# A four-layer graph network on one core: fewer small matmuls, and TensorE's stage work moved to 22 common lots

## What is computed

```python
# layer 0: additive attention; adj is both the projection W and the score bias
s1 = h @ W1.T; s2 = h @ W2.T                       # 256 features each
pre = s1[:, :, None, :] + s2[:, None, :, :] + b_lin
e = einsum('bije,e->bij', leaky_relu(pre, 0.2), a) + adj
x = x + sigmoid(softmax(e, axis=2) @ h)
# layer 1: xh = elu(h @ Wi + bi); e = sigmoid(tgt_i + src_j + be) * mask
# recv = elu(concat(e @ xh, xh * rowsum(e)) @ Wn + bn)
# x = x + concat(recv, xh) @ Wm + bm
# layer 2: attention exp(8 tanh(q k / 8 sqrt(d))) * adj, normalised, times h and v
# layer 3: five steps of a gated recurrent unit over messages adj @ h
```

## Time and profile before

| | before |
|---|---|
| median of three runs | 5996.21 us |
| profiled execution: time | 5989.9 us |
| profiled execution: span from first to last instruction | 5988.1 us |
| TensorE's granted clock, mean | 0.996 |
| PE (TensorE matmuls) busy | 98% |
| ACT (ScalarE) busy | 88% |
| POOL (GpSimd) busy | 82% |
| DVE (VectorE) busy | 81% |
| DMA traffic | 36.62 MB, 6 GB/s on average |

### The profile page before, as it was taken

The page is one execution under the profiler, slowest core; times in us unless marked ns, Lnnn a source line. Parts: engine busy times, 40 slices in busy tenths (PEclk is TensorE's granted clock), DMA queues, the critical chain, the costliest instruction groups (busy, mean ns, idle before and its releaser), DMA issues.

```text
span 5988.1 us, 128923 instructions
## 1 busy us (share of the span) xinstructions
PE 5885.9 (98%) x41812; PEld 2318.3 (39%) x41812; DVE 4837.7 (81%) x9171; ACT 5269.2 (88%) x12793; POOL 4916.4 (82%) x10392
## 2 busy tenths in 40 slices
PE   8999999999999999999999999999999999999997
PEld 2333333333334333333333333333433333333334
DVE  8978887888887888878888788888888887888873
ACT  8988898899988899888999889998889988899983
POOL 9988888888888888888888888888888888888880
PEclk9999999999999999999999999999999999999998
DMA  0000000000000000000000000000000000000000
GB/s 13 5 3 7 7 7 6 3 6 7 7 6 3 7 6 7 7 2 7 6 7 7 6 3 6 7 7 6 3 7 6 7 6 3 7 6 7 7 5 6
DMA packets 44353, 36.62 MB, mean 6 GB/s; under 512 B 4721, under 2 KB 39410, under 8 KB 43506
## 3 DMA queue, kind: packets, MB, share of 16 engines
q1 hardware_dynamic: 43506, 26.50, 1.5%
HBM read 9.71 MB, written 8.39 MB: 3 GB/s over the span
## 4 chain that ended last, share of the span: by engine, by line
PE 94%; ACT 2%; DVE 1%; POOL 1%; issue 1%; DMA 0%; SPq 0%; POOLq 0%; ACTq 0%; DVEq 0%
PE S L1015 58%; PE R L957 15%; PE S L957 6%; PE W L957 5%; PE R L1157 3%; PE PA L957 2%; ACT ring L812 2%; PE R L1165 1%; POOL ring L507 1%; PE PB L957 1%; PE S L1006 1%; PE S L1008 1%; DVE ring L613 1%; PE PB L1042 1%; PE PA L1023 0%
## 5 line engine op out<-in xcount | busy, mean ns | idle before, releaser
L507 POOL TENSOR_SCALAR ring<-W,U 128x256 f32<-128x256 f32 x9664 | 4686.4, 503 | 713.8 <-PE S L1015 642.2
L812 ACT ACTIVATE ring<-W,U 128x256 f32<-128x256 f32 x10272 | 4244.1, 503 | 13.3 <-PE S L1015 13.2
L1015 PE MATMUL S<-ring,a_window 128*32 128x512 f32 x32768 | 3750.1, 596 | 12.8 <-POOL ring L507 7.3
L613 DVE TENSOR_TENSOR ring<-U,W 128x512 f32<-128x512 f32 (+1 forms) x3840 | 3209.2, 862 | 155.5 <-PE S L1015 117.4
L1015 PEld LDWEIGHTS S<-ring,a_window 128*32 128x32 f32 x32768 | 952.2, 110 | 2269.6 <-issue 2245.4
L608 DVE TENSOR_TENSOR ring<-U,W 128x256 f32<-128x256 f32 x2464 | 993.6, 408 | 0.0
L957 PE MATMUL R<-mT,W 128*128 128x512 f32 (+1 forms) x640 | 339.1, 611 | 2.7 <-ACT mT L916 2.7
L957 PE MATMUL R<-AT,h 128*128 128x256 f32 x1260 | 316.8, 395 | 2.7 <-ACT h L928 2.1
L748 DVE SCALAR_TENSOR_TENSOR rh<-tr,h3T 128x512 f32<-128x512 f32 (+1 forms) x165 | 114.1, 692 | 240.2 <-ACT tr L919 240.2
L957 PEld LDWEIGHTS R<-AT,h 128*128 128x128 f32 x1260 | 230.4, 193 | 129.7 <-issue 100.6
L478 POOL TENSOR_TENSOR minus_mean<-mv,minus_one 128x4 f32<-128x4 f32 (+1 forms) x160 | 31.6, 197 | 272.3 <-DVE mv L676 216.8
(11 more groups left out here) (186 smaller groups left out, 4238.6 us busy)
## 6 DMA issues: line engine op xcount, KB each, us to landing
X<-in_x SPq DMA_DIRECT2D x64, 128.0 KB, 2.4
X_held<-X SPq DMA_DIRECT2D x32, 256.0 KB, 2.3
out<-OUT SPq DMA_DIRECT2D x64, 128.0 KB, 1.9
raw<-in_L_gnn_w_w SPq DMA_DIRECT2D x3, 128.0 KB
A<-in_adj SPq DMA_DIRECT2D x1, 256.0 KB, 2.7
Wn<-in_L_gnn_Wn SPq DMA_DIRECT2D x1, 128.0 KB
Wm<-in_L_gnn_Wm SPq DMA_DIRECT2D x1, 128.0 KB
rawu<-in_L_gnn_u_w SPq DMA_DIRECT2D x2, 64.0 KB
```

The lines of the kernel that those rows point to most:

```text
L507: last = gp.tensor_scalar(ring[:, place, g, half * N:(half + 1) * N], W[:, y, c], LARGEST, U[:, y, c, i:i + 1], ALU.min, ALU.max)
L613: piece = dve.tensor_tensor(ring[:, place, g:g + groups].rearrange("p g (h j) -> p g h j", h=NB), u.unsqueeze(3).to_broadcast([P, groups, ...
L812: last = act.activation(ring[:, place, g, half * N:(half + 1) * N], W[:, y, c], ACT.Relu, bias=U[:, y, c, i:i + 1], scale=-1.0)
L1015: last = pe.matmul(S[y][g * ROWS:(g + 1) * ROWS, :], a_window[:, c, ROWS - 1 - row:2 * ROWS - 1 - row], ring[:, place, g], start=False, st ...
```

## The change

1. **Layer 0's linear terms.** ScalarE's block becomes `Relu(W + U_minus)`, with `U_minus = -U` made by VectorE at the stage `evacuate`. That is the maximum less U of node i, and a term of node i alone drops out of the softmax over j. So `lin_w` is one matrix for all, one matmul with 512 columns replaces the two of `lin_w` and the one of `A_bias`, and `w_lin`, `lin_i`, `exp_bias`, `by_max` and its memsets go. A is added in VectorE's pass that finds the maximum, with one `tensor_tensor_reduce` per 256 columns that writes -(S + A) to SBUF and its minimum; ScalarE's exponential reads that.
2. **Layer 1.** GpSimd adds bm to X1 ahead of time (`X1_shifted`) and adds the two halves of the edge weights (`edge_sum`); the four matmuls with `bm_half` go, and the four of `ones` become one with 512 columns, behind a wait for GpSimd.
3. **Tables.** All stage tables move. POST and PRE get one table for each half of the turn. Distinct lots with a TensorE stage go from 34 to 22. The first matmul of a half comes on top: in the second half it stood in the same gap as a stage (table place 66, done after lot 63), now it stands alone. The planner gets 26 units more of GpSimd work, and the shares of a turn's 1024 blocks go from 401, 302 and 321 (VectorE, GpSimd, ScalarE) to 403, 298 and 323.

```diff
-POST = dict(score=5, exp=6, transpose=10, copy=11, aggregate=12, tanh=14, residual=15)
-PRE = dict(stats=40, norm=43, transpose=46, copy=49, project=57, evacuate=61)
-LN1 = dict(stats=17, norm=19, transpose=20, copy=23)
-L1 = dict(project=26, exp=28, elu=29, edge_terms=31, edge_copy=33, tanh=33, mask=36, aggregate=39, agg_copy=42, receive=44, recv_exp=45, recv_elu=47, out=49, residual=52)
-LN2 = dict(stats=56, norm=59, transpose=68, copy=70)
-L2 = dict(project=74, copy=77, scores=80, tanh=84, exp=85, mask=88, aggregate=94, residual=99)
-LN3 = dict(stats=2, norm=5, transpose=9, copy=10)
-L3_AT, L3_PERIOD = 12, 22
+POST = (dict(score=5, exp=6, transpose=10, copy=11, aggregate=14, tanh=16, residual=17),
+        dict(score=5, exp=6, transpose=12, copy=13, aggregate=16, tanh=18, residual=19))
+PRE = (dict(stats=40, norm=43, transpose=46, copy=49, project=58, evacuate=61),
+       dict(stats=40, norm=43, transpose=48, copy=50, project=56, evacuate=60))
+LN1 = dict(stats=19, norm=21, transpose=24, copy=26)
+L1 = dict(shift=23, project=32, exp=34, elu=35, edge_terms=40, edge_copy=42, tanh=42, mask=45, halves=46, aggregate=49, agg_copy=51, receive=54, recv_exp=55, recv_elu=56, out=58, residual=60)
+LN2 = dict(stats=62, norm=65, transpose=68, copy=70)
+L2 = dict(project=76, copy=78, scores=84, tanh=86, exp=87, mask=90, aggregate=98, residual=101)
+LN3 = dict(stats=2, norm=5, transpose=10, copy=11)
+L3_AT, L3_PERIOD = 14, 22
...
+    put(pool, L1, 0, shift=13, halves=13)
...
+                if t == L1["shift"]:
...
+                    need(gp, x2_ready, turn.at(1, -1))
+                    gp.wait_ge(x1_ready, turn.at(2, 0))
+                    gp.tensor_tensor(X1_shifted[:], X1[:], bm_half[:].unsqueeze(1).to_broadcast([P, 4, P]), ALU.add).then_inc(x1_shifted, 1)
+                if t == L1["halves"]:
+                    gp.wait_ge(edge_ready, pair)
+                    gp.tensor_tensor(edge_sum[:].rearrange("p (y n) -> p y n", y=2), edge[:, :, 0], edge[:, :, 1], ALU.add).then_inc(edge_halves, 1)
...
-                if p == PRE["evacuate"]:
-                    dve.wait_ge(uw_psum, value)
-                    dve.tensor_copy(lin_i[:, y], PA[:, N:N + NB])
+                if p == PRE[1 - y]["evacuate"]:
+                    dve.wait_ge(u_ready, value)
+                    dve.tensor_scalar(U_minus[:, y], U[:, y], -1.0, None, ALU.mult).then_inc(u_minus_ready, 1)
...
                     dve.wait_ge(freed[RING - 1], lots_done)
-                    dve.tensor_reduce(neg_max[:], S[y][:].rearrange("p (r j) -> p r j", r=NB), AXIS.X, ALU.max,
-                                      negate=True).then_inc(max_ready, 1)
-                    one_piece()
-                    dve.wait_ge(max_ready, value)
-
+                    need(dve, prob_ready, value - 1)
+                    dve.memset(score_carrier[:], 0.0)
                     for r in range(NB):
-                        last = dve.scalar_tensor_tensor(exp_bias[:, r:r + 1], neg_max[:, r:r + 1], lin_i[:, y, r:r + 1],
-                                                        lin_i[:, y, r:r + 1], ALU.subtract, ALU.add)
-                    last.then_inc(exp_bias_ready, 1)
+                        last = dve.tensor_tensor_reduce(neg_score[:, r], S[y][:, r * N:(r + 1) * N], A[:, r], -1.0, LARGEST,
+                                                        ALU.add, ALU.min, accum_out=neg_max[:, r:r + 1])
+                    last.then_inc(max_ready, 1)
...
-                    act.wait_ge(u_ready, turn.at(2, y + 1))
+                    act.wait_ge(u_minus_ready, turn.at(2, y + 1))
...
-                                          bias=U[:, y, c, i:i + 1], scale=-1.0)
+                                          bias=U_minus[:, y, c, i:i + 1])
...
-                    for r in range(NB):
-                        pe.matmul(S[y][:, r * N:(r + 1) * N], lin_w[:, y, r], H0T[:, y], start=r == 0, stop=False,
-                                  skip_group_check=True)
-                    pe.matmul(S[y][:].rearrange("p (r j) -> p r j", r=NB), ident[:], A_bias[:], start=False, stop=False,
+                    pe.matmul(S[y][:].rearrange("p (r j) -> p r j", r=NB), lin_w[:],
+                              H0T[:, y].unsqueeze(1).to_broadcast([P, NB, N]), start=True, stop=False,
                               skip_group_check=True)
...
-                    for r in range(NB):
-                        mm(PA[:, N + r:N + r + 1], H0T[:, y, r * P:(r + 1) * P], w_lin[:, 0:1])
...
-                    for y in range(2):
-                        for r in range(NB):
-                            last = mm(S[1][:, y * N:(y + 1) * N], ones[:], edge[:, y, r], r == 0, r == NB - 1)
-                    last.then_inc(agg1_psum, 1)
+                    pe.wait_ge(edge_halves, pair)
+                    mm(S[1][:], ones[:], edge_sum[:]).then_inc(agg1_psum, 1)
...
-                        mm(S[1][:, n * P:(n + 1) * P], ones[0:1, :], bm_half[:], True, False)
-                        mm(S[1][:, n * P:(n + 1) * P], recvT[:, n * P:(n + 1) * P], Wm[:, 0], False, False)
+                        mm(S[1][:, n * P:(n + 1) * P], recvT[:, n * P:(n + 1) * P], Wm[:, 0], True, False)
```

More of the change, by code:

```diff
@@ L85, in put @@
             costs[at + table[name]] += cost
[L87 to L92, removed]
+    for h in range(2):
+        half = h * LOTS_B
+        put(vector, POST[h], half, score=7, transpose=1.5, residual=3.4)
+        put(scalar, POST[h], half, exp=10, copy=4.8, tanh=5)
+        put(vector, PRE[h], half, stats=5.5, evacuate=0.6)
+        put(scalar, PRE[h], half, norm=5, copy=2.6, evacuate=12)
+        put(pool, PRE[h], half, stats=20)
     for ln in (LN1, LN2, LN3):
@@ L131, in spare_blocks @@
     spare = [0] * LOTS
-    for half in (0, LOTS_B):
-        for at in (POST["score"], POST["transpose"], PRE["stats"]):
-            spare[half + at] += 1
+    for h in range(2):
+        for at in (POST[h]["score"], POST[h]["transpose"], PRE[h]["stats"]):
+            spare[h * LOTS_B + at] += 1
     for at in (LN1["stats"], LN2["stats"], LN3["stats"], L1["elu"], L1["recv_elu"], L2["residual"]):
@@ L172, in node @@
     return half * P + g * ROWS + row
[L175 to L181, removed]
 def gnn_stack(nc, x, adj, L0_b, L0_a, L1_Wi, L1_bi, L1_We, L1_be, L1_Wn, L1_bn, L1_Wm, L1_bm, L2_q, L2_k, L2_v,
@@ L258, in gnn_stack @@
         Wm = sb("Wm", [P, 2, P])
-        bm_half = sb("bm_half", [1, P])
+        bm_half = sb("bm_half", [P, P])
         cols = sb("cols", [P, 7])
@@ L275, in gnn_stack @@
         U = sb("U", [P, 2, EC, N])
+        U_minus = sb("U_minus", [P, 2, EC, N])
         W = sb("W", [P, 2, EC, N])
-        lin_i = sb("lin_i", [P, 2, NB])
         ring = sb("ring", [P, RING, GROUPS, NB * N])
@@ L287, in gnn_stack @@
         neg_max = sb("neg_max", [P, NB])
-        exp_bias = sb("exp_bias", [P, NB])
         row_sum = sb("row_sum", [P, NB])
@@ L463, in _ @@
                              pattern=[[-1, P]], channel_multiplier=1).then_inc(gp_const, 1)
-            gp.memset(by_max[:], 1.0).then_inc(mask_ones, 1)
-            gp.wait_ge(mask_ones, 1)
-            for y in range(2):
-                for c in range(EC):
-                    for n in range(BLOCKS):
-                        g, half = group_half(n)
-                        for first, end in scalar_runs(y, c, n):
-                            last = gp.memset(by_max[:, c, y, half, g * ROWS + first:g * ROWS + end], 0.0)
-            last.then_inc(mask_set, 1)
             gp.wait_ge(dve_const, 1)
@@ L517, in body @@
                         blocks(turn, t)
-                    if p == PRE["stats"] and turn.has_main and (y == 0 or turn.pre_next):
+                    if turn.has_l12:
+                        layer1(t, turn)
+                    if p == PRE[y]["stats"] and turn.has_main and (y == 0 or turn.pre_next):
                         pre(turn.at(2, y + 2))
@@ L996, in lot @@
                 if p == 0:
-                    need(pe, prob_ready, turn.at(2, y - 1))
+                    need(pe, max_ready, turn.at(2, y - 1))
                     if y == 0:
@@ L1106, in layer2 @@
                     pe.wait_ge(hT_ready[1], pair)
-                    pe.wait_ge(prob_ready, turn.at(2, 1 if turn.has_main else 0))
+                    pe.wait_ge(max_ready, turn.at(2, 1 if turn.has_main else 0))
                     mm(S[0][:], G[:], h2T[:])
```

100 lines of the change are left out of this document (45 added, 55 removed).

## The result

The changed kernel takes 5821.18 us in the median (5805.18 to 5829.51), the kernel before beside it 5998.4: a ratio of 0.970 with a 95% interval of 0.967 to 0.973. The forecast was 5730, range 5700 to 5800. The direction was right and the size was not: 266 us were forecast and 177 came. The profiled execution took 5805.18 us (span 5803.3), against 5989.9 before and 5724 forecast for it.

A forecast was written before the change was run, and what follows sets the result against it. TensorE, busy 98% of the span, was taken as the bound: 30 turns x 9.0 us = 270, plus 8 at the edges, less 12 for stalls, net 266, so 5996.2 becomes 5730 us; range 5700 to 5800.

The forecast's parts named there:

- The working of TensorE's time: Steady turn on TensorE: fewer matmuls and merged visits remove 9.0 us, bounds 7.9 and 9.4.
- The linear terms: Layer 0's visit on TensorE: one 512-column matmul remains, 0.86 us goes twice, 1.72 us a turn.
- the output stage: TensorE's stage of 4.21 us loses the `bm_half` matmuls: 2.2 us goes, leaving about 2.
- the merged visits: TensorE's stage visits: 11 fewer a turn at 0.30 us each, 3.3 us, between 2.2 and 3.7.
- GpSimd's wait for the ring: GpSimd's wait for TensorE to free a ring place: down from 21.4 us a turn to about 10.
- The wait for `edge_halves`: TensorE behind its lot 46: costed at nothing; forecast wrong if it ends a TensorE wait.
- the gap at the turn's change: TensorE before a looped turn's first matmul: the prediction gave it no term and no rival.
- The sign of being wrong that I had set: Profile after: forecast wrong if steady turns are over 179 us; 175 to 176 us expected.
- what VectorE's operations cost: VectorE in a steady turn: grows by at most some 2 us, to 152.5.
- the rival "GpSimd is held by VectorE": U_minus on VectorE may hold GpSimd's blocks some 1 us a turn; no change of the sum, no chance given.
- The term of 0.4 us a turn: Turn's change, lots 0 to 8: ScalarE's lead touches zero, costing 0.4 us a turn, bounds 0 and 3.
- the producers' rival (0.11): ScalarE at 94% becomes a second bound: TensorE loses up to 3 us a turn, 5808; chance 0.11.

The follow-up runs named there:

- experiment 12: Changed kernel with four turns a pass, layer 3 gate values in PSUM, 128 waits, later GpSimd statistics, now half_inv on ScalarE: 5697.32 us, ratio 0.950.
- experiment 4: Changed kernel with the stage tables of before (34 lots with a stage), the new matmuls kept: 5892.38 us, ratio 0.983.
- Experiment 1: Changed kernel with four turns written out in each pass of the loop (7 passes instead of 29): 5754.27 us, ratio 0.960.
- experiment 2: Changed kernel with 128 already fulfilled waits put ahead of TensorE's loop: 5761.96 us, ratio 0.961.
- experiment 5: Kernel before with 296 fulfilled waits at the head of TensorE's stream, which moves its loop: 6095.85 us, ratio 1.017.
- experiment 7: Changed kernel with four turns a pass, 128 waits ahead of the loop and layer 3's gate values in PSUM together: 5722.75 us, ratio 0.954.
- experiment 3: Changed kernel with layer 3's candidate, z gate and gated difference left in PSUM: 5773.12 us, ratio 0.963.
- experiment 11: Changed kernel, one turn a pass, with 216 waits, gate values in PSUM and GpSimd's LayerNorm 3 statistics two lots later: 5739.51 us, ratio 0.958.

## Why the prediction was wrong

**Right.** The working of TensorE's time held. Its work in a steady turn was to fall by 9.0 us, from 183.03 to 174.03; in the turns of experiment 12 that follow no return it is 174.03. (In the changed kernel it is 175.15, with what lies behind the return.) The linear terms take 1.05 us in place of 1.92, and the output stage 1.78, where I had 2.0. The matmuls alone give 5.7 x 30 + 8 less 2.7 x 28 for the dearer return, 103, and experiment 4 measured 104; the merged visits save 3.3 a turn. GpSimd's wait for the ring fell from 21.4 to 5.7 us a turn, where I had about 10. ScalarE has 164.55 us against 165. The wait for `edge_halves` does not show among TensorE's waits, nor that for U_minus among ScalarE's.

**The step that failed: the gap at the turn's change, taken as staying as it was.** The timeline showed [1.11 <-issue] before the first matmul, with no engine that ends it. I passed over it, since the change removes nothing there: the sum has no term for it, and the chances of the forecast and its rivals leave it no room. It is what TensorE pays for the jump back, and it hung on how the stream of instructions lies, which every edit of that stream alters. It went from 1.35 to 3.9 us, 70 of the 80 us missing in the turns. Experiment 1 shows that it is tied to the jump, experiments 2 and 5 that moving the stream alone shifts it by tens of microseconds either way, with one packet of instructions a turn less or more. The sign of being wrong that I had set, turns over 179 us, was not met (178.4), though PE at 98% was missed as well (97%).

**The second step: what VectorE's operations cost.** The sum had at most 2 us a turn for it, and the rival "GpSimd is held by VectorE" had the direction one way only: VectorE holds GpSimd, which has room. It also goes the other way. Once GpSimd stops less for the ring (its 21.4 us of waiting were gaps), VectorE's operations with two SBUF operands are held beside its blocks. VectorE went from 150.5 to 156.2 us and TensorE stood 0.65 us a turn at lot 72. The new operations were priced well (0.82 us for the two reductions against 0.9, U_minus 517 ns within 0 to 690).

**The term of 0.4 us a turn** was put at lots 0 to 8 with ScalarE as the one that is late. Nothing of the kind happened: in three turns that I worked out, ScalarE was 3 to 7 us ahead there, VectorE 2.7 to 5.7 and GpSimd 1.5 to 7, with the gap at the return to give them time. Where there is no return (experiments 1 and 7) a stall appears, 1.2 us of idle time a turn, on GpSimd. So the producers' rival (0.11) was right in that they come next, wrong in the engine. Its price of 5808 lies near the result, by accident.

**Smaller.** GpSimd's additions cost 1.36 and 1.30 us, not 1.2, within the bounds. The Trainium skill, page "GPSIMD Engine Reference", section 3.1 (elementwise), would give an estimate of 1.1; the rows are some 20% above it. Turn 1 rose by 1.2 us where 1.5 less was forecast. The median stands 16 us above the profiled execution, not 6, at a lower mean granted clock (experiment 3). The range's lower end was 5706 by its own terms (5996 - 282 - 8), not 5700.

**Still open in part** is why a return costs 1.35 us in one program and 2.1, 2.8, 3.0, 3.6, 3.9, 4.05 or 4.8 in others. Two things sort most of it. Taking only the returns at full clock, the programs that fetch 12 packets a turn pay 1.35 (the kernel before), 1.7 (experiment 11), 1.9 and 2.05 us (128 and 216 waits); those that fetch 13 pay 3.2 (the kernel before with 296 waits), 3.5, 3.7 and 3.9 (experiment 3, the changed kernel, experiment 4). Returns with a stretch at half clock cost 0.9 to 2.0 us more in the changed kernel and the four with waits. What decides between 12 and 13, and why the gap alone is 1.1 us in one program and 2.0 in another, no run here shows.

## What to carry to other kernels

A gap marked "issue" behind a loop's jump is a term of the sum with bounds of its own, whenever an edit changes how many instructions stand ahead of or in the loop; here it was worth more than the stall that I looked for. The count of instruction packets and the mean granted clock on the page tell whether it changed. When the engine that bounds a kernel gets faster, look at which engine's idle gaps vanish and who used them: here VectorE used GpSimd's. And a fix of one stall moves the next one a few lots on, so the leads have to be read again after each.

## What the runs showed of the hardware

- A loop's return on TensorE cost between 1.35 and 4.8 us in kernels whose turns are alike. 296 waits that are met at once, ahead of the loop, made the kernel before 100 us slower (12 or 13 packets of instructions a turn became 13); 128 made the changed one 59 us faster (13 became 12). The loss does not all lie at the jump: there were stalls of 1.91 us behind the first four matmuls, of 0.54 us in lot 0, and of 0.7 us spread over the 59 matmuls behind it.
- Behind a gap at a return TensorE's granted clock fell to half for some microseconds, after 22 of 28 returns in the kernel before with 296 waits, after 14 in the changed one with 128, after one in the kernel before. It cost 2.0 and 1.8 us each time in the first two.
- VectorE's operation on two SBUF operands can be held over several of GpSimd's blocks: `diff` took 3.09 us amid 42 blocks, 688 ns in the mean with one operand in PSUM. So can one of two elements, 1.73 us amid 32 blocks; on ScalarE it takes 214 ns.
- Waits that are met at once delayed the start of the first lot by 12 us (296 of them), 8 us (216) and 3 us (128).
